# Cross attention with its context tokens grouped 512, 512, 512 and 65 in place of 384, 384, 384 and 449

## The reference

```python
def _mha(q_in, k_in, v_in, Wq, Wk, Wv, bv, causal):
    q = jnp.einsum('bsd,hde->bhse', q_in, Wq)
    k = jnp.einsum('btd,hde->bhte', k_in, Wk)
    v = jnp.einsum('btd,hde->bhte', v_in, Wv) + bv[None, :, None, :]
    scores = jnp.einsum('bhse,bhte->bhst', q, k) * scale
    ...
    p = jax.nn.softmax(scores, axis=-1)
    o = jnp.einsum('bhst,bhte->bhse', p, v)
...
ca = _mha(x, encoder_output, encoder_output, Wq2, Wk2, Wv2, bv2, causal=False)
```

## Time and profile before

| what | value |
|---|---|
| median of 3 runs | 1624.4 us (1619.35 to 1627.89) |
| profiled execution | 1628.24 us |
| its span, first to last instruction | 1626.8 us |
| TensorE busy | 1495.2 us, 92% |
| VectorE, ScalarE, GpSimd busy | 56%, 41%, 16% |
| cross attention's projections and rounds | from 88 to about 957 us of the span |
| one sequence's 8 rounds in the steady part | about 105 us |
| mean granted TensorE clock | 0.952 |

### The profile page before, as it was taken

The page is one execution under the profiler, slowest core; times in us unless marked ns, Lnnn a source line. Parts: engine busy times, 40 slices in busy tenths (PEclk is TensorE's granted clock), DMA queues, the critical chain, the costliest instruction groups (busy, mean ns, idle before and its releaser), DMA issues.

```text
span 1626.8 us, 28472 instructions
## 1 busy us (share of the span) xinstructions
PE 1495.2 (92%) x12052; PEld 1149.4 (71%) x12052; DVE 907.5 (56%) x1338; ACT 668.8 (41%) x1217; POOL 256.0 (16%) x171
## 2 busy tenths in 40 slices
PE   7799999999999999999988877968997799999998
PEld 3479888877787878778777665853597476666665
DVE  3633423544535354454465435357677478888886
ACT  1424432443444344334345433423321246666664
POOL 1213211110201010211121415020252100000000
PEclk9889999999999999999999987988888789999999
DMA  7013110110101010101111345032000029999992
GB/s 245 2 43 95 59 43 21 43 40 21 43 21 43 21 40 27 37 27 37 40 43 40 105 180 182 1 124 108 1 1 27 0 104 338 345 346 343 344 340 90
DMA packets 86780, 163.15 MB, mean 100 GB/s; under 512 B 4608, under 2 KB 27136, under 8 KB 86144
## 3 DMA queue, kind: packets, MB, share of 16 engines
q1 hardware_dynamic: 86656, 161.34, 28.7%
HBM read 160.28 MB, written 1.05 MB: 99 GB/s over the span
## 4 chain that ended last, share of the span: by engine, by line
PE 86%; DVE 9%; issue 2%; ACT 1%; POOL 1%; DMA 0%; ACTq 0%; DVEq 0%
PE ring L591 18%; PE ring L581 16%; PE ring L1787 8%; PE turnbank L625 6%; PE pv L1811 4%; PE sc L608 3%; PE pv L644 3%; PE sc L1065 3%; PE sc L1452 3%; PE pv L1787 3%; PE pv L1819 2%; PE sc L1475 1%; PE ring L1074 1%; PE pv L653 1%; DVE nm L813 1%
## 5 line engine op out<-in xcount | busy, mean ns | idle before, releaser
L549 POOL TENSOR_TENSOR x_l<-raw,x_h 128x1536 fp32r<-128x1536 f32 (+1 forms) x44 | 158.9, 3613 | 739.5 <-ACT x_h L543 739.5
L1636 DVE TENSOR_TENSOR w_lo<-w_raw,w_hi 128x2048 fp32r<-128x2048 f32 x88 | 200.4, 2284 | 25.1 <-ACT w_hi L1877 25.0
L731 ACT ACTIVATE prob<-sc,nm 128x384 f32<-128x384 f32 (+1 forms) x256 | 153.9, 611 | 119.5 <-DVE nm L818 80.6
L581 PE MATMUL ring<-x_h,wk_h 128*128 128x384 f32 (+1 forms) x512 | 186.5, 364 | 5.4 <-POOL x_l L549 5.4
L591 PE MATMUL ring<-wv_h,x_h 128*128 128x512 f32 (+2 forms) x520 | 191.4, 368 | 0.0
L813 DVE TENSOR_REDUCE nm<-sc 128x2 f32<-128x898 f32 (+1 forms) x128 | 127.9, 1020 | 105.1 <-PE sc L608 105.0
L591 PE MATMUL ring<-wv_h,x_l 128*128 128x512 f32 (+2 forms) x520 | 181.4, 349 | 0.0
L591 PE MATMUL ring<-wv_l,x_h 128*128 128x512 f32 (+2 forms) x520 | 181.1, 348 | 0.0
L581 PE MATMUL ring<-x_h,wk_l 128*128 128x384 f32 (+1 forms) x512 | 177.2, 346 | 0.0
L581 PE MATMUL ring<-x_l,wk_h 128*128 128x384 f32 (+1 forms) x512 | 176.8, 345 | 0.0
L1877 ACT CAST w_hi<-w_raw 128x2048 fp32r<-128x2048 f32 x88 | 167.6, 1907 | 18.4 <-PE pv L1811 15.5
(11 more groups left out here) (450 smaller groups left out, 2643.9 us busy)
## 6 DMA issues: line engine op xcount, KB each, us to landing
w_raw<-in_ew SPq DMA_DIRECT2D x96, 1024.0 KB, 5.5
raw<-in_ctxT SPq DMA_DIRECT2D x33, 768.0 KB, 4.3
raw<-in_ctxT SPq DMA_DIRECT2D x11, 900.0 KB, 4.7
wf<-in_wf SPq DMA_DIRECT2D x2, 4096.0 KB, 19.0
xin<-in_x SPq DMA_DIRECT2D x1, 1024.0 KB, 5.6
w_in<-in_wq SPq DMA_DIRECT2D x1, 1024.0 KB, 7.8
w_in<-in_wk SPq DMA_DIRECT2D x1, 1024.0 KB, 10.1
w_in<-in_wv SPq DMA_DIRECT2D x1, 1024.0 KB, 12.2
```

The lines of the kernel that those rows point to most:

```text
L549: pool.tensor_tensor(x_l[x % 3][:, :, 0:w], raw[x % 3][:, :, 0:w], x_h[x % 2][:, :, 0:w].bitcast(F32), ALU.subtract)\
L581: m = pe.matmul(ring[k % 2][:, 0:w], wt[:, c, e:e + P], xt[:, c, 0:w], start=c == 0 and n == 0, stop=c == NC - 1 and n == 2)
L731: act.activation(prob[:, i, 0:WIDTHS[r]], sc[:, i, score_columns(r)], ACT.Exp, bias=nm[:, b % 2, r, h:h + 1], accum_out=psum[:, b % 2, r, ...
L1636: return eng.tensor_tensor(w_lo[n % NSLOT][:, :, :], w_raw[n % NSLOT][:, :, :], w_hi[i % 4][:, :, :].bitcast(F32), ALU.subtract)
```

## The change

The group boundaries move to 512, 1024 and 1536 tokens, so that the fourth group has 65 tokens (66 columns with the spare one) and its own four key jobs of 12 matmuls. A group now holds four value tiles, the fourth group only the 13th. The number of loads (44), jobs (258) and matmuls stays. The slots are no longer filled by the number of jobs but by a weight, `job_columns`: the columns for a key job, at least 128; 512 or 300 for a value job.

```diff
-    GROUPS = ((0, W0), (W0, W0), (2 * W0, W0), (3 * W0 - 1, W1 + 1))
+    GROUPS = ((0, 512), (512, 512), (1024, 512), (1535, 66))
...
     def tile_group(i):
-        r, j, _ = VTILES[i]
-        return j if r == 0 else 3 - j
+        return i // 4
...
+    def job_columns(k):
+        job = JOBS[k]
+        if job[0] == "k":
+            return max(GROUPS[LOADS[job[1]][1]][1], 128)
+        return 512 if job[4] is None else 300
+
     def slots_of(n):
         return 3 if n % 2 else 4
 
     for first_, last_, rounds_ in SEGMENTS[1:]:
         slots = [(n, s) for n in rounds_ for s in range(slots_of(n))]
+        total, done = sum(job_columns(k) for k in range(first_, last_)), 0
         for k in range(first_, last_):
-            n, s = slots[(k - first_) * len(slots) // (last_ - first_)]
+            n, s = slots[int((done + job_columns(k) / 2) * len(slots) / total)]
+            done += job_columns(k)
             PLAN[n][s].append(k)
```

## The result

The changed kernel takes 1686.4 us (median of 4 runs, 1683.4 to 1689.4) where the kernel before takes 1626.1 beside it: 60 us more, a ratio of 1.038 (95% interval 1.034 to 1.042). Page of after: span, busy time, the chain's shares, loads.

The account below looks back on a forecast made before the run. TensorE's queue was taken to bound the kernel, busy 92% of the span. Terms 27 + 13 + 3 - 4 + 2 + 3 + 1.5 gave +45.5 us, 1670 us against the median 1624.4; range 1646 to 1692.

Parts of the forecast that it names:

- the two large terms: In cross attention on TensorE: key matmuls held to their weight load, +27 us, and slots without a job, +13 us.
- Key jobs: Cross attention's key matmuls: a 66-column one costs its weight load, about 111.6 ns, so each key block +0.84 us; +27 us.
- the columns rival: Key jobs: a short matmul costs by its columns, key term -5, sum +14, 1638 us; chance 0.05.
- Empty slots: Rounds of cross attention: 12 more slots without a job, each waiting 1.12 us around VectorE's copy; +13 us.
- Rounding at a sequence's end: ScalarE at 7 sequence ends: larger rounding ahead of the last transposes' copy delays outputs 0.44 us more each; +3 us.
- Waits covered by longer jobs: TensorE's 6 waits for exponentials ahead of transposes, 4.1 us, shrink as key jobs grow by 0.66 us; -4 us.
- Short jobs in a row: A sequence's last round: three or four short key jobs each wait for an earlier job's copy; +2 us.
- The dense start: Round 0 and round 3: few, short jobs leave ScalarE standing for a load, copies queued behind; +3 us.
- The sparse end: Rounds 56 to 60: load, rounding and subtraction outlast TensorE's few jobs, waits 6.9 instead of 5.4 us; +1.5 us.

Follow-up runs that it names:

- The pair of runs with 66 and 256 columns: Changed kernel with slots filled by number of jobs as before, short key jobs streaming 66 columns (1692.4 us) or 256 (1680.9 us).

## Why the prediction came out right, and what it missed

The time, 1686, lies in the range, and the two large terms were right in mechanism and about right in size. But the sum of +45.5 us was 15 short of +60, and the clock, which nobody had thought of, cost about as much as what was missing. That the range took it in is luck.

**Key jobs, +27.** Right. A short matmul takes 111.7 ns, where 111.6 was taken from a row of another stage, and the columns rival (1638) is out. The jobs' time by rows is the 27; taken away in place they give back 23, some of it clock.

**Empty slots, +13.** Right, a little low: 13 us for ten of them in the old kernel, where 13 was for twelve.

**Rounding at a sequence's end, +3.** The place was right, the size was not. Moved away, 16 us come back in the changed kernel, some of it clock (at half for 34 us instead of 48). But the kernel before gets 4 to 7 us back too when its own rounding is moved, so that of the difference between the two kernels some 9 to 12 us belong here. The waits of the outputs grew by 12.1 - 7.7 = 4.4 us; where the rest lies wasn't followed.

**Waits covered by longer jobs, -4.** Wrong: the waits for exponentials stayed, at 4.3 us (4.1 in the earlier trace rows). The longer jobs are there, but with two roundings in the last round ScalarE is later too, perhaps by as much; that was not tested.

**Short jobs in a row, +2.** No wait: three jobs in 4.02 us are 36 matmuls with no gap, and no wait for the ring stands among those from 208 to 880 us. But the row had another price, below.

**The dense start, +3.** Up to the scores of round 8 the changed kernel needs 11.6 us more, of which the key jobs of two sequences are 2 x 3.4 = 6.7; the other 5 fit the size. The mechanism isn't borne out: from 88 to 208 us most of TensorE's waits are for VectorE's copies (2.7 us, 0.9 before), and those for ScalarE's copies come to 1.3 us in two.

**The sparse end, +1.5.** The chain of load and rounding was right in kind (ScalarE stood 5.5 us in two waits for loads from 880 to 1020 us), but TensorE waited elsewhere than in the earlier trace rows, for a copy held up behind that rounding and not for a subtraction:

```profile
991.64 1.90 ACT L550 CAST x_h<-raw 128x2048 fp32r<-128x2048 f32 x1 [1.57 <-DMA raw<-in_ctxT]
993.45 0.58 ACT L728 COPY pT<-turnbank 128x512 f32<-128x512 f32 x1
...
994.28 0.97 PE L651 MATMUL pv<-pT,v 128*32 128x64 f32 x28 [5.27 <-ACT pT L728]
```

From the scores of round 56 to those of round 63 the changed kernel needs 91.6 us and the one before 83.9; key jobs are some 2 of these 8.

**What was missing: TensorE's clock.** The prediction took the steady part's full clock for granted. The pair of runs with 66 and 256 columns puts 11.5 us, or 14.5 with the 3 that the columns cost, on it where it falls most. Counted from the granted clock between the first and the last scores, the kernel with 66 columns there stands at half clock for 65 us, that with 256 for 21, the changed kernel for 48 and the one before for 7. In proportion, 41 us for those 44, I put 11 to 14 us on the clock, as an estimate.

Key jobs 23 to 27, slots 13, roundings 9 to 12 and the rest of the clock, some 7 to 9 (without the 14 us at half that went with the roundings), make 52 to 61 us beside the measured 60. These shares were not all measured in the changed kernel and may overlap, so this is a sum that fits and not a proof of each of them. From the last scores to the end the kernels differ by 5 us as well, the changed one being the shorter (657.3 against 662.4): the old groups have both values (662.4 in the kernel before, 657.3 with the rounding behind the copy) and so it isn't the change.

## What to carry to other kernels

Cutting a stream into pieces is free only as long as a piece streams for longer than its weights take to load; here 256 columns cost hardly more than 66. Price a matmul by the longer of the two, and look in the trace for the row with the fewest streamed columns. When a regrouping shifts which slot a helper step lands in, follow that step on its own engine's queue: four roundings a sequence cost 41 us here by their place alone, as much behind the copy as ahead of it. A move that frees the steady part can cost elsewhere, as in the dense rounds of the kernel before. And a slot left empty, where a round trip through another engine stands on both sides of it, costs that round trip; but filling all slots is no gain by itself: with the new groups the even filling was no faster (1692 against 1686), with a second rounding of each sequence in a last slot and the clock at half for longer (65 us against 48).

## What the runs showed of the hardware

- Float32r matmuls with 128x128 weights start 111.7 ns apart with 66 columns streamed, and 120 ns with 256: a job of 12 with nearly four times the columns costs 0.1 us more. With 384, 450 and 512 columns it is 0.18, 0.21 and 0.24 us, counted over whole jobs.
- The granted clock fell from 2.4 to 1.2 GHz while TensorE was busy without a gap, behind rows of matmuls that streamed 66 columns (626 to 633 us above: 7.00 of 7.00 us busy, then 0.57). With 256 columns in the same slots it stayed at 0.99 to 1.00 in the steady part, where it had been 0.94 to 0.98. I had expected falls behind idle time alone, as at 920 us of the kernel before, with TensorE busy for 3.99 of the 7 us ahead of it. Not every such row is followed by a fall, and the clock fell as well where there were none: for 24 us with groups of 512, 384, 384 and 321 and the rounding right behind the copy, for 34 us with the short jobs cut to one matmul. The Trainium skill, page "TensorE: Matmul & The Clock Gate", section "Part 1: The HAM clock gate", ties the clock to how busy the engine has been; in this trace it was busy throughout by the profile's count, and the clock fell all the same. As far as the two differ the measurement decides: here the profile's busy share doesn't tell whether the clock stays up.
